# Other tables for weaving three streams of work into five engine queues, on one core

## The reference, cut to what matters

```python
x = L0_attn_x                                   # (8, 512, 128)
xn = _layernorm(x)
s = _L0_attn_ref(xn, ...)                       # 16 heads of causal softmax attention, q and k 8 wide, v 64 wide
g = _silu(_L0_ffn_ref(xn, ...))                 # 8 experts, top 2, capacity 512: over all 4096 rows at once
x = x + s * g
xn = _layernorm(x)
s = _L1_attn_ref(xn, ...)                       # conv, delta rule in chunks of 32 (16 chunks in sequence), decay average
g = _silu(_L1_ffn_ref(xn, ...))                 # 2 layers: local attention over windows of 64, 8 heads, then gated GELU
x = x + s * g
```

## Time and profile before

| | us |
|---|---|
| median of 3 runs | 2554.92 (2554.34 to 2555.77) |
| the profiled execution, its own time | 2570.71 |
| its span, first to last instruction | 2568.6 |
| PE, ACT, DVE, POOL busy in the span | 2057.2, 1389.1, 1351.8, 530.4 |

### The profile page before, as it was taken

One profiled execution on the slowest core, in us unless ns is written; L12 is line 12 of the kernel. 1 busy time (PEld: TensorE's weight loads), 2 busy tenths in 40 slices (PEclk: granted clock), 3 DMA queues, 4 the chain that ended last, 5 costly groups with the idle time before them and its releaser, 6 DMA issues.

```text
span 2568.6 us, 51135 instructions
## 1 busy us (share of the span) xinstructions
PE 2057.2 (80%) x20756; PEld 1172.1 (46%) x20756; DVE 1351.8 (53%) x3137; ACT 1389.1 (54%) x3603; POOL 530.4 (21%) x597
## 2 busy tenths in 40 slices
PE   4597678977797878978797868978798868977677
PEld 3143434454445634555344634555344634554434
DVE  6424474555647374555646364554637465555352
ACT  1644357653867267653767257653767257653343
POOL 2712040302212040302212040301303040301130
PEclk9698579988899789987898779997899878997877
DMA  9124500020001100020101110020100210000000
GB/s 284 54 82 145 132 19 3 1 51 10 10 2 31 21 17 3 1 51 10 10 2 21 32 17 3 1 51 10 9 2 12 41 17 3 1 14 6 1 1 5
DMA packets 129737, 75.93 MB, mean 30 GB/s; under 512 B 76067, under 2 KB 121468, under 8 KB 127454
## 3 DMA queue, kind: packets, MB, share of 16 engines
q1 hardware_dynamic: 125406, 66.34, 10.5%
q0 software_dynamic: 4096, 6.32, 2.0%
HBM read 41.55 MB, written 33.16 MB: 29 GB/s over the span
## 4 chain that ended last, share of the span: by engine, by line
PE 40%; DVE 17%; ACT 15%; issue 9%; POOL 8%; DMA 1%; POOLq 0%; DVEq 0%; SPq 0%; ACTq 0%
PE PS L1406 4%; POOL area_b L1712 4%; PE PS L1269 4%; ACT work_a L786 3%; PE PS L1419 3%; PE PS L585 3%; ACT area_b L1503 3%; POOL area_b L1720 2%; PE PS L1377 2%; PE PS L1304 2%; ACT work_a L803 2%; DVE work_a L913 2%; DVE area_b L1599 2%; PE PS L741 2%; PE PS L1339 2%
## 5 line engine op out<-in xcount | busy, mean ns | idle before, releaser
L1712 POOL TENSOR_TENSOR area_b<-area_b,tables 128x256 f32<-128x256 f32 x256 | 212.9, 851 | 830.7 <-DVE area_b L1599 830.7
L786 ACT ACTIVATE work_a<-PS,work_a 128x512 bf16<-128x512 f32 (+3 forms) x512 | 264.8, 536 | 78.8 <-DVE work_a L913 77.8
L913 DVE TENSOR_REDUCE work_a<-PS 128x2 f32<-128x1024 f32 (+3 forms) x256 | 200.7, 820 | 109.7 <-PE PS L537 109.5
L1503 ACT ACTIVATE area_b<-PS,neg_max 128x192 f32<-128x192 f32 (+1 forms) x512 | 202.2, 417 | 99.3 <-DVE neg_max L1639 76.0
L803 ACT ACTIVATE work_a<-PS 128x1024 f32<-128x1024 f32 (+1 forms) x192 | 169.4, 882 | 136.4 <-PE PS L567 135.8
L1269 PE MATMUL PS<-wqkv,area_b 128*128 128x512 f32 x384 | 200.4, 654 | 11.5 <-DVE area_b L1599 10.2
L1304 PE MATMUL PS<-area_b 64*128 64x192 f32 (+1 forms) x1024 | 158.0, 444 | 64.4 <-ACT shiftT L1489 37.0
L1726 POOL TENSOR_TENSOR rstd_b<-var_eps_b,minus_half 128x4 f32<-128x4 f32 x16 | 16.4, 1025 | 808.3 <-DVE var_eps_b L123 808.3
L585 PE MATMUL PS<-work_a 128*64 128x512 f32 (+3 forms) x1024 | 179.3, 453 | 0.0
L1304 PEld LDWEIGHTS PS<-area_b 64*128 64x128 f32 x1024 | 106.1, 256 | 116.2 <-ACT shiftT L1489 41.5
L1519 ACT ACTIVATE area_b<-PS 128x768 f32<-128x768 f32 (+1 forms) x128 | 97.4, 761 | 103.7 <-PE PS L1347 102.7
(11 more groups left out here) (319 smaller groups left out, 4209.0 us busy)
## 6 DMA issues: line engine op xcount, KB each, us to landing
work_a<-stack_d SPq DMA_DIRECT2D x32, 512.0 KB, 9.2
stack_d<-area_b SPq DMA_DIRECT2D x48, 192.0 KB, 3.1
stack_d<-area_b SPq DMA_DIRECT2D x32, 128.0 KB, 2.7
area_b<-in_L_attn_x_dram SPq DMA_DIRECT2D x4, 512.0 KB, 5.5
slots_in<-work_a SPq DMA_DIRECT2D x8, 256.0 KB, 4.3
stack_d<-work_a SPq DMA_DIRECT2D x4, 512.0 KB, 7.3
work_a<-xnT_d SPq DMA_DIRECT2D x8, 256.0 KB, 3.9
work_a<-in_L_attn_x_dram SPq DMA_DIRECT2D x8, 256.0 KB, 3.0
```

Source lines behind the costliest of these rows:

```text
L786: nc.scalar.activation(dump0[:, n % 2 * T:n % 2 * T + (i + 1) * P], PS[:, a:a + (i + 1) * P], ACT.Exp, bias=neg_max0[:, k:k + 1], accum_ou ...
L913: nc.vector.reduce_max(neg_max0[:, 2 * g * NT + i:(2 * g + 2) * NT:NT], at[:, :, Q_AT[i]:Q_AT[i] + (i + 1) * P], AX_X, negate=True).then_i ...
L1503: nc.scalar.activation(dump2[:, n % 4 * 256:n % 4 * 256 + w], PS[:, a:a + w], ACT.Exp, bias=neg_max2[:, k:k + 1], accum_out=sums2[:, k:k + ...
L1712: nc.gpsimd.tensor_tensor(to[:, n, :, r, :], src[:, n, :, 1 - r, :], table(2 * n + 1, t)[:, 32 * r:32 * r + 32].unsqueeze(1).to_broadcast( ...
```

## The change

All ten tables get other numbers; no instruction, buffer, wait or semaphore changes. Slices without work on an engine have no effect there, so what changes on an engine is the order of those with work:

- SP: nothing. POOL: in each batch `S8` (adding the gathered rows) now stands ahead of B's `a.st` (the norm's reciprocal root), where it stood behind it.
- Head, DVE: `r3` moves from ahead of `v0` to behind `S16`; `p4` from ahead of `D3` to behind `D6`; `p5` from behind `D14` to ahead of `D9`.
- Head, PE: `r4`, which came after `T15`, now comes after `T12`; between it and `e7.2` lie `T13` to `T19` (before: `T16` to `T20`); the order at its end is `e7.2 T20 p1 T21 T22 T23 T24 p2 p3 o0 o1 p4` (before: `e7.2 T21 p1 T22 p2 p3 T23 T24 p4 o0 o1`).
- Head, ACT: `T12 e0 T13 T14 e1 T15 e2 e3 T16 e4 e5 T17 T18 e6 T19 e7 T20 T21 T22 T23 p1 p2 p3 o0 D1 D3 D4 D5 D6 p4 D7 p5` (before: `T14 e0 e1 T15 T16 T17 T18 e2 e3 e4 T19 T20 e5 e6 e7 T21 p1 T22 p2 T23 p3 o0 D1 p4 D3 D4 D5 D6 D7 p5`). DVE ends it with `e7.2 p1 T21 T24 p2 p3 o0` (before: `e7.2 p1 T21 p2 p3 T24 o0`).
- Batches, DVE, start: `a.q2 v0 a.q3 a.q4 a.q5 a.q6 v1 a.q7 a.q8 v2 v3 S0 a.q9 S1` (before: `a.q2 a.q3 a.q4 v0 a.q5 v1 a.q6 v2 a.q7 a.q8 v3 S0 S1 a.q9`), and `a.s4` ahead of `S4` (before: behind `S5`).
- Batches, PE: `a.s4` and `a.s5` ahead of `S4` (before: behind `S5` and `S7`); `a.tr` behind `T3`, `a.w2` behind `T7`, `b.in` behind `T9` (before: `T6`, `T10`, `T12`); `b.q3` to `b.q6` some two slices earlier; `b.s1` ahead of `D1`, `b.s2` ahead of `D2`; the end is `b.t8 D16 b.wo D17 b.st D18 b.tr b.h0 D19 b.h1 b.h2 b.w2 D20` (before: `b.t8 b.wo b.st D16 b.tr D17 b.h0 b.h1 D18 b.h2 D19 b.w2 D20`). DVE: `b.s5` ahead of `D7` (before: behind it).

```diff
--- before.py
+++ after.py
@@ -2216,43 +2216,43 @@
 
 
         A_AHEAD_OF_HEAD = {
-            "tensor": (0, 0, 0, 0, 0, 0, 0, 0, 0, 0, 0, 0, 1, 45, 45, 45, 45, 45, 45, 48, 48, 48,
-                48, 48, 48, 48, 48, 48, 49, 50, 50, 50, 50, 50, 50, 50, 50, 50, 51, 52, 52, 54, 65, 68,
-                71),
-            "scalar": (0, 0, 0, 0, 0, 0, 0, 0, 0, 0, 0, 0, 3, 44, 44, 44, 44, 44, 44, 47, 48, 48,
-                48, 48, 48, 48, 48, 48, 49, 50, 50, 50, 50, 50, 50, 50, 51, 51, 51, 52, 54, 59, 64, 66,
+            "tensor": (0, 0, 0, 0, 0, 0, 0, 0, 0, 0, 0, 1, 17, 42, 42, 44, 44, 44, 44, 44, 45, 46,
+                46, 46, 46, 46, 46, 46, 46, 46, 46, 46, 49, 49, 49, 49, 49, 49, 50, 54, 54, 56, 65, 65,
+                70),
+            "scalar": (0, 0, 0, 0, 0, 0, 0, 0, 0, 0, 0, 3, 6, 40, 42, 42, 42, 44, 44, 44, 45, 45,
+                45, 45, 46, 46, 46, 46, 46, 46, 46, 48, 48, 48, 49, 49, 49, 52, 53, 53, 54, 63, 64, 69,
+                83),
+            "vector": (0, 0, 0, 0, 0, 0, 0, 0, 0, 0, 0, 0, 22, 36, 39, 40, 40, 41, 41, 41, 42, 44,
+                44, 45, 45, 47, 47, 47, 47, 47, 47, 49, 49, 49, 49, 49, 49, 49, 49, 54, 54, 63, 65, 72,
+                76),
+            "gpsimd": (0, 0, 0, 0, 0, 0, 0, 0, 0, 0, 0, 0, 1, 2, 6, 7, 8, 8, 8, 8, 11, 13,
+                13, 14, 14, 22, 22, 23, 23, 26, 28, 32, 32, 32, 44, 45, 52, 53, 56, 56, 59, 64, 64, 77,
                 77),
-            "vector": (0, 0, 0, 0, 0, 0, 0, 0, 0, 0, 0, 0, 0, 40, 41, 41, 41, 41, 41, 44, 45, 45,
-                45, 45, 45, 45, 45, 45, 45, 46, 46, 46, 46, 46, 48, 48, 49, 49, 50, 53, 53, 58, 72, 72,
-                76),
-            "gpsimd": (0, 0, 0, 0, 0, 0, 0, 0, 0, 0, 0, 0, 2, 31, 31, 32, 32, 36, 36, 37, 40, 40,
-                40, 40, 40, 40, 40, 41, 42, 43, 43, 43, 44, 45, 52, 52, 53, 59, 65, 65, 65, 71, 71, 71,
-                71),
-            "sync": (0, 0, 0, 0, 0, 0, 0, 0, 0, 0, 0, 0, 0, 33, 33, 33, 33, 33, 33, 34, 37, 37,
-                38, 38, 38, 38, 38, 38, 39, 39, 39, 39, 39, 39, 39, 39, 39, 39, 39, 39, 42, 51, 80, 86,
-                89),
+            "sync": (0, 0, 0, 0, 0, 0, 0, 0, 0, 0, 0, 0, 17, 41, 44, 45, 45, 45, 45, 47, 47, 47,
+                48, 50, 51, 51, 51, 51, 51, 51, 51, 51, 51, 51, 52, 52, 52, 56, 56, 56, 60, 60, 72, 82,
+                92),
         }
         A_AHEAD_OF_B = {
-            "tensor": (93, 93, 94, 94, 94, 94, 95, 96, 96, 100, 101, 101, 102, 102, 104, 106, 107, 107, 109, 110, 112, 113,
-                115, 116, 118, 119, 120, 122, 123, 129, 132, 133, 133, 133, 135, 138, 140, 144, 145, 145, 147, 147, 149, 149,
-                150, 151, 152, 154, 154, 157, 158, 158, 160, 164, 165, 165, 165, 165, 165, 165, 165, 165, 165, 166, 167, 167,
-                168, 169),
-            "scalar": (77, 83, 83, 93, 94, 94, 95, 95, 96, 99, 100, 101, 102, 102, 104, 106, 106, 107, 108, 109, 111, 113,
-                114, 115, 117, 118, 122, 122, 126, 129, 132, 132, 132, 133, 137, 138, 142, 144, 144, 145, 147, 150, 150, 150,
-                151, 152, 152, 156, 158, 159, 159, 159, 159, 163, 164, 165, 165, 165, 165, 165, 165, 165, 165, 166, 167, 167,
-                168, 169),
-            "vector": (93, 93, 93, 93, 93, 94, 95, 96, 96, 100, 101, 101, 101, 102, 104, 106, 106, 107, 109, 111, 112, 112,
-                116, 118, 119, 120, 120, 122, 123, 131, 131, 131, 131, 131, 132, 140, 141, 144, 144, 145, 147, 147, 147, 149,
-                151, 152, 153, 155, 156, 157, 158, 158, 158, 163, 164, 164, 165, 165, 165, 165, 165, 165, 166, 167, 167, 167,
+            "tensor": (93, 93, 94, 94, 94, 94, 95, 95, 96, 100, 100, 101, 101, 102, 102, 102, 106, 107, 108, 110, 112, 113,
+                115, 116, 118, 120, 120, 122, 123, 126, 128, 129, 130, 130, 132, 138, 140, 141, 142, 144, 145, 147, 149, 149,
+                149, 149, 151, 154, 156, 157, 158, 158, 158, 162, 162, 162, 162, 162, 162, 162, 165, 166, 167, 168, 168, 169,
                 169, 169),
-            "gpsimd": (71, 71, 71, 72, 73, 73, 77, 77, 77, 77, 77, 77, 77, 77, 78, 78, 85, 87, 94, 95, 95, 95,
-                95, 96, 96, 96, 96, 105, 106, 108, 108, 111, 118, 118, 118, 118, 118, 118, 118, 118, 118, 119, 119, 125,
-                125, 126, 127, 133, 133, 135, 136, 136, 138, 142, 143, 143, 143, 143, 145, 145, 146, 146, 156, 160, 160, 160,
-                162, 162),
-            "sync": (109, 109, 109, 109, 109, 111, 117, 123, 127, 127, 133, 138, 139, 139, 139, 140, 140, 140, 140, 140, 140, 141,
-                141, 141, 145, 145, 145, 145, 145, 145, 145, 145, 145, 145, 145, 148, 148, 148, 148, 148, 148, 148, 148, 154,
-                156, 159, 166, 166, 166, 168, 168, 168, 173, 180, 181, 181, 182, 182, 189, 189, 189, 189, 189, 191, 191, 192,
-                197, 199),
+            "scalar": (87, 93, 93, 93, 94, 94, 95, 95, 95, 99, 100, 100, 101, 101, 101, 104, 105, 107, 108, 110, 111, 112,
+                114, 115, 118, 119, 120, 120, 123, 126, 129, 129, 129, 130, 136, 138, 139, 141, 142, 144, 145, 149, 150, 150,
+                150, 151, 151, 156, 157, 157, 157, 158, 158, 158, 159, 159, 159, 159, 159, 161, 162, 165, 166, 168, 168, 170,
+                177, 178),
+            "vector": (93, 93, 93, 94, 94, 94, 94, 95, 95, 99, 100, 101, 101, 102, 102, 103, 106, 106, 108, 110, 115, 116,
+                116, 118, 120, 120, 120, 122, 124, 129, 129, 129, 130, 130, 133, 138, 139, 140, 140, 141, 146, 147, 148, 149,
+                152, 152, 152, 155, 156, 156, 158, 158, 158, 164, 164, 164, 164, 164, 164, 164, 165, 166, 167, 168, 168, 169,
+                169, 169),
+            "gpsimd": (87, 87, 87, 87, 89, 89, 89, 90, 90, 90, 91, 91, 95, 95, 97, 97, 97, 97, 98, 99, 99, 102,
+                102, 103, 103, 103, 103, 103, 107, 108, 108, 108, 109, 109, 109, 109, 109, 110, 123, 123, 123, 123, 129, 137,
+                137, 137, 137, 138, 139, 140, 141, 141, 141, 143, 151, 151, 151, 151, 151, 152, 152, 156, 166, 173, 176, 176,
+                176, 180),
+            "sync": (111, 113, 113, 113, 114, 114, 116, 123, 130, 133, 133, 138, 138, 142, 142, 142, 145, 145, 145, 145, 145, 146,
+                146, 146, 146, 146, 146, 146, 146, 146, 146, 147, 148, 155, 156, 156, 159, 166, 167, 172, 172, 172, 172, 175,
+                175, 175, 175, 175, 175, 175, 175, 177, 181, 184, 185, 188, 188, 191, 191, 192, 192, 192, 192, 192, 194, 196,
+                201, 204),
         }
 
         def slices(engine):
```

## The result

The changed kernel takes 2535.2 us (median of four runs, 2530.3 to 2537.9), the kernel before 2554.6 in the same comparison (2554.0 to 2555.8): ratio 0.9907, 95% interval 0.9888 to 0.9926. It is faster by 19.5 us.

What follows compares the result with a forecast made beforehand. PE was taken as busiest (2057.2 of 2568.6 us), with order and waits setting the head, so gains lay only in periods' holes and the clock. Median 2554.9 + 10.1 (head) + 0 (periods) = 2565 us, range 2544 to 2583.

Steps and rivals of the forecast that it cites:

- the head: Opening stretch with A of batch 0: +10.1 us, bounds +5 and +16.
- the periods: Seven stretches, A of one batch beside B of the one before: 0 each, bounds -3 and +2.5 us.
- the periods win: Rival, chance 0.28: a.s4 hides in S4's wait for gathered rows, -2.5 us a period, 2547.5 us in all.
- Step 1: Period's start: v2, v3 behind a.q8 on DVE make PE's v3, S0, S1 2.9 us later, B's s0 about 2.5.
- Step 2: Period's gather: a.s4, a.s5 fill DVE's unmoved 5.25 us wait, but the late start eats the gain: +1.1 at a.t2.
- Step 3: Period's full PE stage: a.tr behind T3 waits some 0.7 us for the layer norm, +1.8 us at b.q1.
- Step 4: Period's q slices of b: o1 on DVE stands behind b.q8's unchanged POOL chain, the 1.8 us are absorbed, 0.
- Step 5: Period's delta rule: b.s5 ahead of D7 on DVE delays D7, D8 and the triangle, +1.1 us.
- Steps 6 and 7: Period's end: reordered D16 to D18 give 0, PE being full; the clock at layer b's hidden matmuls -1, bounds 0 and -2.9.

Runs made afterwards that it cites:

- the pair: The main comparison of the kernel before and the changed kernel, with one profiled trace of each: 2554.6 us before, 2535.2 after.
- e12: The changed kernel again, unedited, on a chip where the kernel before takes 2554.7 us: 2535.0 us.
- e1: Kernel before with only the head's table new, periods old: 2629.1 us against 2623.0 for the kernel before.
- e15: Kernel before with only the gather's counts new (a.s4 to a.t2 on PE, ACT, DVE): 2577.8 us, ratio 1.0112, kernel before at 2554.7.
- e8: Kernel before with only the gather's counts new (a.s4 to a.t2 on PE, ACT, DVE): 2655.0 us, ratio 1.0114, on a slower chip.
- e14: Kernel before with the periods' table new from b.q2 on (q slices of b, delta rule, end): 2516.9 us against 2554.7.
- e13: Kernel before with the periods' table new from b.q9 on (delta rule and end): 2528.1 us, ratio 0.9906.
- e9: Kernel before with the periods' table new from b.q2 on (q slices of b, delta rule, end): 2577.1 us against 2624.0.
- e3: Kernel before with only the end of the periods new (b.wo to b.w2, all engines): 2603.1 us, ratio 0.9924.
- e7: Kernel before with only the end of the periods new (b.wo to b.w2), repeated: 2603.1 us, ratio 0.9912.
- e11: Kernel before with only D18 moved ahead of b.h0 on PE: 2667.5 us against 2624.0.
- e4: Kernel before with the periods' table new except its end (b.wo to b.w2), head old: 2644.8 us, ratio 1.0076.
- the fourth set: The last four follow-up runs (e12, e13, e14, e15), on one chip where the kernel before takes 2554.7 us.

## Why the prediction was wrong

The forecast was +10.1 from the head and 0 from the periods. The head's number was near, in part by luck; the first stages of a period were near; the q slices of b and the end of the period were not.

**The head.** Right in its mechanism up to `o0`. `T12` ends at 148.2 (forecast 146.6), ACT's first copy of `p1` comes at 218.9 (220.0), DVE's `o0` at 233.6 (235.8), and the whole comes to +11.8 (10.1). ACT and DVE of the changed kernel, beside the earlier trace rows:

```profile
218.88 1.07 ACT L1966 CAST area_b<-PS 128x512 bf16<-128x512 f32 x2
...
230.38 1.07 ACT L1966 CAST area_b<-PS 128x512 bf16<-128x512 f32 x2 [3.72 <-DMA stack_d<-area_b]
```

```profile
233.58 0.28 DVE L885 TENSOR_SCALAR work_a<-area_b,work_a 128x128 f32<-128x128 f32 x1
...
248.94 0.75 DVE L959 TENSOR_SCALAR work_a<-PS,conv_w 128x512 f32<-128x512 f32 x1 [3.39 <-PE PS L614]
```

`o0` begins 3.2 us after `p3`'s first copy, and POOL's last gather had ended at 225.6: `p3` decides, as I said. Three terms are off. From `p1`'s to `p3`'s first copy it is 11.5 us, not 12.6. And `D3` starts 15.4 us after `o0` (17.1 before), 1.8 earlier against it, as forecast (-1.7), and waits for PE. The third is what lies behind `p4`. I had the whole +10.1 reached at `D7`'s copies and 0 from there on; the traces have +8.2 at the end of those copies, +9.1 at the start of the triangular solve, +9.8 at its end, +10.1 behind `D17` and +11.8 at the end of A. So 1.9 too much up to `D7` stood against 3.6 that I had put at nothing, most of it SP's way through DRAM and the products behind it. The size also varies more than I allowed for the one number: +11.8 in the pair, +4.4 and about +6 in the later runs (`e12`, `e1`); +4.4 is below my lower bound of +5.

**The rival "the periods win"** came nearest to the measured time (2547.5), and its mechanism is refuted: it took the filled wait for the rows as the gain, -2.5 a period. Alone that move costs 23.1 us on the kind of chip that I forecast for, and 28.4 on the other (`e15`, `e8`).

**Steps 1 to 3 of a period.** Step 1: `a.s0` on PE is 0.7 us later on average, not 2.5. Step 2 said that `S4`'s wait "itself does not move" and has 5.25 us. It has 0.46 to 5.35, 20.1 in seven batches, and PE's scores for `a.s4` come late enough to put `S4` behind them in every period. At `a.t2` I had +1.1, the traces have -0.3. Step 3: from `a.t2` to `b.q1` +1.6 (forecast +1.8 less 1.1, so +0.7). At `b.q1` the sum is +1.3 where I had +1.8: near, by two errors against each other.

**Step 4** failed too, by less. Forecast: the 1.8 us are absorbed. In the traces 2.0 are: `o1` ends 0.7 us earlier than before. The runs show more. `e14` is 11.2 us below `e13` by this step alone, and there is nothing to absorb there, since everything ahead is in the old order. So the order of the q slices is a gain of its own, 11.2 / 7 = 1.6 us a period. I had argued that `b.q8`'s chain over POOL "ends at the same time"; but from `b.q1` to the end of `o1` the new order takes 32.6 us (`e9`) for 34.4 (`e1`), so the chain must start earlier too.

**Step 5.** +1.1 forecast for the delta rule; from `o1`'s to `b.t8`'s end the traces have -0.7. No run has this stage alone; `e13` (-26.7) with it and `e3`, `e7` (-19.9, -23.5) without it, on different kinds of chip, leave it near 0 or a small gain.

**Steps 6 and 7 are the ones that failed.** "PE is full either way: 0", and "the clock: -1, bounds 0 and 12 x 0.243 = -2.9". I had 1 us a period for both; the end alone gives 19.9 and 23.5 us, 2.8 to 3.4 a period, and in the pair's traces 6.4. I had the right suspicion, that the granted clock falls to 1.2 GHz where the hidden part runs, and put it too low, in three ways.
- I priced only the twelve hidden matmuls. They went from 853 to 610 ns, exactly the -2.9 of my outer bound. But in the same trace `b.w2` was at 0.61 too (8.0 us, now 5.2), and `D17` took 4.1 us for 2.7 on average. By the earlier trace rows the clock was 0.81 over a stage of 35.3 us; the whole stage at 2.4 GHz, 0.19 x 35.3 = 6.7 us (an estimate from that row), is what I should have taken as the bound, for my -2.9.
- I read "full" as an argument that nothing could be won. Busy time at 1.2 GHz can shrink with no work taken out: PE's shrank by 46.9 us between the two traces.
- I took the clock's fall as given in its place and asked what lies in it. The traces show that the order also sets whether it comes and how long it lasts: 17 us with `D18` ahead of the hidden part (`e11`), 7 or 10 in the old order, and in the new one none in 28 of 63 periods and 3 or 7 us in 28 more.

**What part is luck.** In one and the same order of the end, `b.w2` takes 7.7 us on average in the trace before, 5.2 to 5.8 in `e1`, `e4` and `e8`, and 6.4 in `e15`. The profiled execution of the kernel before is 16 us above its median, and (7.7 - 5.4) x 6 = 14, the first period having 5.2 in any case. I take it that its timed executions had `b.w2` mostly at 2.4 GHz; that is an estimate, no run shows it. So some 2.3 of the 6.4 us a period that the pair's traces show at the end belong to that one execution. Of the rest the runs of the fourth set give an account: the table from `b.q2` on is worth 37.8 us, 5.4 a period (`e14`), the whole change 19.7 (`e12`), so head, start, gather and full stage together cost 18.1. The head costs 4.4 to 11.8 of these, which leaves 6 to 14 us for the three stages, although the gather's counts alone cost 23.1 (`e15`).

**Why the chips differ.** In the changed kernel `S4` moves by +3.2 us on a 2624 chip, where DVE is held up during POOL's issues, and by +1.0 in the pair. 2.2 x 7 = 15 us, most of the 17.7 between -19.7 and -2.0. That is an estimate from the place of one instruction.

**Against the forecast's tests.** "Wrong I would be if the periods moved by more than 2 us each: then a stage of the period has more slack than I gave it, or the clock fell elsewhere." It was the second, and the first in the q slices.

**What stays open.** Why one kind of chip holds DVE up while POOL issues indirect transfers and the other doesn't. Why q slices and delta rule together bring 23 to 27 us more than the end alone on the 2624 chips (`e9` against `e3` and `e7`), and the q slices 11 on the other. Why the clock falls at about 237 us of a period in the new order and at 245 in the old, and in some periods not at all. And `D17` and `D18` without `D16`, the start alone, and the end alone on a 2555 chip weren't tried.
